# Moving the pauses of a gather queue to the borders of its work units

## The reference, cut to what matters

```
q, k, v = x @ Wq + bq, x @ Wk + bk, x @ Wv + bv      # 4 heads of 32
attn    = einsum('nhc,mhc->hnm', q, k) / sqrt(32)
alpha   = softmax(attn where adj != 0)               # over the neighbours m of node n
out     = einsum('hnm,mhc->nhc', alpha, v)
x_r     = x @ Ws + bs
beta    = sigmoid([out, x_r, out - x_r] @ Wb)
result  = layernorm(x + beta * x_r + (1 - beta) * out)
```

## Time and profile before

| | us |
|---|---|
| median of 3 runs (lowest, highest) | 1948.49 (1945.45, 1970.56) |
| profiled execution | 1964.78 |
| its span in the trace | 1962.9 |
| busy: POOL, DVE, PE, ACT | 1174.4, 1310.3, 1164.9, 839.9 |
| first and last gather on POOL, start | 66.5, 1936.1 |
| last result store on POOL, start | 1953.0 |

### The profile page before, as it was taken

The page is one execution under the profiler, slowest core; times in us unless marked ns, Lnnn a source line. Parts: engine busy times, 40 slices in busy tenths (PEclk is TensorE's granted clock), DMA queues, the critical chain, the costliest instruction groups (busy, mean ns, idle before and its releaser), DMA issues.

```text
span 1962.9 us, 20126 instructions
## 1 busy us (share of the span) xinstructions
PE 1164.9 (59%) x4696; PEld 680.4 (35%) x4696; DVE 1310.3 (67%) x3389; ACT 839.9 (43%) x1595; POOL 1174.4 (60%) x1711
## 2 busy tenths in 40 slices
PE   7322746657574756466655657756766668444553
PEld 5101433334342334233323334423423334233342
DVE  5876878666756776557656468757555677886564
ACT  2331443334643463344634348545635476431112
POOL 4454565566566656656566656565665665676664
PEclk9565677677776776667777578876667767666565
DMA  9947856666755776564866668776767778433331
GB/s 334 354 164 199 318 198 233 214 233 223 293 197 183 258 271 234 216 218 161 342 230 215 247 243 294 265 258 247 252 217 278 249 255 280 140 89 96 94 89 57
DMA packets 130037, 438.70 MB, mean 223 GB/s; under 512 B 26567, under 2 KB 61198, under 8 KB 97150
## 3 DMA queue, kind: packets, MB, share of 16 engines
q1 hardware_dynamic: 76510, 297.15, 41.1%
q0 software_dynamic: 52832, 136.07, 22.5%
q10 hardware_dynamic: 576, 4.19, 0.5%
HBM read 417.93 MB, written 19.44 MB: 223 GB/s over the span
## 4 chain that ended last, share of the span: by engine, by line
POOL 34%; issue 24%; DVE 13%; DMA 13%; PE 7%; DVEq 4%; another core or an unknown queue 3%; ACT 2%; SPq 1%; ACTq 0%; POOLq 0%
POOL s_kv L799 31%; DMA s_kv<-kv_rows,s_rec_in 11%; DVE s_raw L1248 2%; DVE s_kv L1246 2%; PE s_acc L1001 1%; DVEq L1296 1%; DVE s_wtop L1295 1%; POOL node_records L766 1%; POOL out_rows L775 1%; ACT s_mask L1023 1%; DVEq L1443 1%; DVE s_kv L1272 1%; DVE s_d_max L1454 1%; PE s_ps_key L889 1%
## 5 line engine op out<-in xcount | busy, mean ns | idle before, releaser
L799 POOL DMA_INDIRECT s_kv<-kv_rows,s_rec_in x1023 | 1024.3, 1001 | 700.6 <-DMA s_kv<-kv_rows,s_rec_in 340.6
L829 PE MATMUL s_ps_w<-s_mask,s_bit_w 128*128 128x512 bf16 x1008 | 374.6, 521 | 332.4 <-ACT s_mask L1023 233.8
L1023 ACT ACTIVATE s_mask<-s_adj_in 128x2048 bf16<-128x2048 f32 x252 | 478.2, 1900 | 114.5 <-DMA s_adj_in<-in_adj 66.7
L1001 PE MATMUL s_acc<-s_kv,ident 128*128 128x128 f32 x2032 | 321.3, 330 | 109.9 <-DVE s_kv L1272 62.8
L1001 PEld LDWEIGHTS s_acc<-s_kv,ident 128*128 128x128 f32 x2032 | 312.2, 244 | 137.4 <-DVE s_kv L1272 77.3
L829 PEld LDWEIGHTS s_ps_w<-s_mask,s_bit_w 128*128 128x128 bf16 x1008 | 111.3, 120 | 559.1 <-ACT s_mask L1023 294.9
L1246 DVE TENSOR_TENSOR s_kv<-s_kv,s_ps_q 128x1536 f32<-128x1536 f32 (+15 forms) x76 | 147.1, 1935 | 235.2 <-DMA s_kv<-kv_rows,s_rec_in 224.3
L1272 DVE TENSOR_TENSOR s_kv<-s_kv,s_ps_q 128x1536 f32<-128x1536 f32 (+15 forms) x76 | 146.7, 1931 | 17.9 <-ACT s_ps_q L1062 10.1
L1062 ACT ACTIVATE s_ps_q<-s_sc 128x56 f32<-128x56 f32 (+17 forms) x76 | 16.7, 220 | 318.4 <-DVE s_sc L1262 218.5
L1248 DVE TENSOR_REDUCE s_raw<-s_kv 128x48 f32<-128x1536 f32 (+15 forms) x76 | 147.1, 1935 | 5.6
L1050 ACT COPY s_xs<-s_ps_x 128x128 f32<-128x128 f32 x63 | 16.6, 264 | 288.7 <-remote 160.4
(11 more groups left out here) (281 smaller groups left out, 1563.2 us busy)
## 6 DMA issues: line engine op xcount, KB each, us to landing
s_adj_in<-in_adj SPq DMA_DIRECT2D x248, 1024.0 KB
s_kv<-kv_rows,s_rec_in POOLq DMA_INDIRECT x1023
kv_rows<-s_kv SPq DMA_DIRECT2D x16, 512.0 KB, 7.6
s_rec_in<-node_records SPq DMA_DIRECT2D x55, 106.0 KB
s_kv<-in_x_cols SPq DMA_DIRECT2D x4, 1024.0 KB, 8.4
s_adj_in<-in_adj ACTq DMA_DIRECT2D x4, 1024.0 KB
s_d_in<-in_x_cols SPq DMA_DIRECT2D x8, 512.0 KB
s_d_v<-kv_rows SPq DMA_DIRECT2D x8, 512.0 KB
```

What stands on the lines that cost most here:

```text
L799: nc.gpsimd.indirect_dma_start(out=kv[0:n, START[k] + s], out_offset=None, in_=kv_dram[:, :], in_offset=bass.IndirectOffsetOnAxis(ap=rec_i ...
L829: last = nc.tensor.matmul(w[:], bit_w[:, slab], mask[:, k % 2, s * WORD:(s + 1) * WORD], start=False, stop=(slab == SLABS - 1))
L1001: last = nc.tensor.matmul(acc[:, c * D:(c + 1) * D], ident[:], kv[:, START[k] + s, D:2 * D], start=(s == 0), stop=(s == plain(k) - 1))
L1023: nc.scalar.activation(mask[:, q % 2], adj_in[:, q % ADJ_RING], ACT.Sign, accum_out=edges[:, t, h:h + 1]).then_inc(masked, 1)
```

## The change

The pauses get other places. A unit is cut into `PIECES[k]` = ceil(HELD[k] / 14) pieces of nearly the same size, and POOL considers a pause only ahead of a piece (and, as before, ahead of a scatter and of a store): it pauses where the piece would not fit in what is left of 14. No unit has over 28 gathers, so a unit has one or two pieces.

```
--- before.py
+++ after.py
@@ -80,7 +80,7 @@
 NODE_AT = D + TOP
 DEGREE_MAX = 1023
 GATHER_US = 1.3
-RUN = 12
+RUN = 14
 SCAN_US = 15.0
 LEAD = 4
 BEHIND = 6
@@ -114,6 +114,14 @@
 
 
 HELD = [plain(k) + (k in FOLD_UNITS) for k in range(len(UNITS))]
+PIECES = [-(-s // RUN) for s in HELD]
+
+
+def piece_at(k, s):
+    return next((-(-(HELD[k] - s) // (PIECES[k] - i)) for i in range(PIECES[k])
+                 if s == sum(HELD[k] // PIECES[k] + (j < HELD[k] % PIECES[k]) for j in range(i))), 0)
+
+
 WINDOW_OF = {t: w for w, tiles in enumerate(WINDOWS) for t in tiles}
 
 
@@ -794,7 +802,8 @@
                     col, n = LIST_AT + first_slot(p, c) + s, rows_with(p, first_slot(p, c) + s)
                     if s == plain(k):
                         col, n = FOLD_AT, P
-                    pause_after(1)
+                    if piece_at(k, s):
+                        pause_after(piece_at(k, s))
                     begun["last"] = (k, s)
                     nc.gpsimd.indirect_dma_start(
                         out=kv[0:n, START[k] + s], out_offset=None, in_=kv_dram[:, :],
```

## The result

The change made the kernel slower: 2019.62 us (median of 4 runs, 1984.46 to 2042.13) against 1957.38 (median of 4 runs of the kernel before beside it, 1945.45 to 1970.56), ratio 1.020 with a 95% interval of 1.013 to 1.028. So the change costs time beyond the noise; whether it is more than 2% is open in this measurement. The forecast was 1898 us and a range that ended at 1940. The profiled execution of after took 1984.46 us, its span is 1982.6 us, 19.7 us over the span of before.

What follows compares the result with a forecast made beforehand. POOL, issuing transfers or pausing, was taken as the bound. Savings of 54.6 us where DVE waits and 12 at the end, less 14 for dearer borders, gave 52 us less: 1898 us from the 1948.5 median, range 1864 to 1940.

Steps and rivals of the forecast that it cites:

- 108 pauses, ten of them free: POOL's pauses go from 97 to 108; ten have later transfers issued or an already awaited gather, costed at nothing.
- The prices: Each POOL pause costed by its place with the old kernel's mean prices: 280.6 us in place of 371.3.
- 280.6 and 14: Forecast pause cost, plus 14 us back because borders behind a store, nearer the adjacency burst, cost 2.5 for 1.79 us.
- direct borders: Pauses at the border of two units with nothing issued in between, priced at 3.54 us each up to 1660 us.
- behind a store: Border pauses with one store issued after the unit's last gather, priced at 1.79 us, 2.5 for 19 of them.
- place does not matter: Rival: only transfers issued since count; direct pauses cost 4.17 us, a store takes off 1.30; 1916 us, chance 0.16.
- burst rival: Rival: shorter units put borders into SP's adjacency loads, 5.67 us direct, 5.56 behind a store; 1997 us, chance 0.08.
- POOL's lead: From 1447 to 1884 us POOL gets up to 21.5 us ahead, sparing DVE 12 us of its wait at the end.
- Nobody but POOL's own transfers holds POOL up for long: Reading of the old profile: POOL either issues, 1.30 us a transfer, or pauses.
- DVE takes it all: In three stretches where DVE waited for gathers 197.1 us, POOL's whole 54.6 us saving shortens the run.
- DVE, or the scan behind it, takes over: Rival: DVE's waits vanish and its list work comes into the open; half the gain stays, 1930 us, chance 0.14.
- The page's rule: Opposing rule: every wait for a landing pays about 2.0 us fixed, 2.3 us per 128 KB gather, wherever it stands.

Runs made afterwards that it cites:

- every 14: The kernel before with RUN = 14, a pause at every fourteenth transfer (83 pauses for 97): 1903.47 us, 0.971 times before.
- borders 12: The changed kernel with RUN = 12, 126 pauses, in two versions: border pauses behind the store 1.016 times before, ahead of it 1.029.
- one back: The kernel before, same 97 pauses, each waiting for the gather before the last, so one can still be in flight: 1.056 times before.

## Why the prediction was wrong

*108 pauses, ten of them free.* Right. The ten cost 0.3 us together.

*The prices.* Their sum was right within 6 us, if an idle time is cut at the landing: 280.6 and 14 make 294.6 us, measured 300.7. Uncut, as the forecast had measured the kernel before (371.3), the same idle times come to some 379 us, since the waits for records and slots stand in them. By class, up to 1660 us, cut at the landing: inside units 26 at 4.30 us (forecast 4.62), direct borders 25 at 4.22 (3.54), behind a store 32 at 1.84 (1.79 for 13, 2.5 for 19), and 24.4 us later (18.2). The "place does not matter" rival had 4.17 us for direct borders and units, which fits, but 2.87 behind a store, which does not: a store in between is worth 2.4 us, not 1.30. Of the burst rival a small part came: 0.68 us on 25 direct borders, 17 us, in line with the busy DMA engines at 885 us; its price of 5.67 us did not.

*POOL's lead.* "Right" was to be DVE's wait for gathers near 165 us; it is 104.6 us. "Wrong" was to be POOL's pauses down by 60 us or more with the end hardly moved, and that came, with the end later.

*The step that failed* is "Nobody but POOL's own transfers holds POOL up for long", carried over to the changed kernel, with "DVE takes it all" built on it. I priced a pause only as time that POOL loses. The term missing from my sum is what a full pause gives to the other engines; I put it at nothing, without a reason. It measured +85 us of other waits in the first trace of after and +169 in the second, against 67 us of forecast gain. What went wrong in the plan is not the number of transfers between two pauses (14 at most in pieces, as the rule says) but what a pause behind a store waits for: the gather issued before the store, and not the store. The cheapest class of the earlier trace rows was cheap because it did not wait for the queue to run empty (ahead of the store the pauses cost 65 us more together), and the change raised it from 9 pauses to 32 up to 1660 us. Between two moments with nothing in flight there were at most 24 transfers in before and 37 in after, and over 16 of them 5 times before, 15 times after.

*The rivals.* "DVE, or the scan behind it, takes over" named the right side: the chain goes from POOL to DVE and PE. Its mechanism was not this one (DVE's busy time is what it was, 1311.6 us, and PE's is lower, 1137.5 us), and it had no way to come out slower.

*The page's rule.* The Trainium skill, "DMA: Bandwidth & Descriptors", "Anatomy of one DMA - SWDGE (gpsimd) path", would have made 11 more pauses cost 25 us. The late direct pauses agree with it again (2.19 us for its 2.3), but all pauses together became 63 us cheaper; that the span grew by about as much (19.7 us) is chance.

**Shown**: at the same cost of pauses, 300 us, other waits are 25 us where a pause falls at every fourteenth transfer and 108 to 193 us where most stand behind stores (after), and putting after's border pauses ahead of the stores makes it faster. Beyond every 14, fewer or shorter full pauses make the others' work later by more than they save. **Argued only**: that it is the truly empty queue that counts, and not just how long POOL stands idle. For it speak after against every 14, with 16 and 6 flights over 25 us at the same idle time, and the table, where at most 8 such flights go with 13 to 34 us of other waits and 9 and more with 93 to 602. But the bound of 25 us was chosen afterwards, and in the three pairs with like numbers of pauses (after and its version ahead of the store, borders 12, before and one back) the idle time changed too, by 65, 63 and 159 us. **Not shown**: that the slow gaps and the 29.65 us of ACT are late loads of instructions. For it speaks only the cause "issue", with one instruction at a time; against it, the instruction packets named above. **Open**: what holds the other engines up; why 15 transfers (9 flights over 25 us, 161 us) do so much worse than 14 (6 flights, 25 us) and no worse than after; why after spread from 1984 to 2042 us on one chip; and what made three of four executions of the pause ahead of the store longer than the traced one.

## What to carry to other kernels

Before you move or cheapen a wait, ask what the rest of the chip does while it lasts. Look up what each pause leaves in flight, and count the longest stretch without a full pause before and after the change. Where pauses serve to empty a queue, first try their number with their form kept: RUN from 12 to 14, one constant, gained what the new rule was meant to gain. And cut an idle time at the moment at which its first cause was over, or a price per pause also contains the waits of others.

## What the runs showed that I had not expected

- Other engines can be held up while POOL's queue of gathers does not run empty: PE at one instruction in 1.4, 2.1 or 2.8 us (16 such matmuls took 1.87 us otherwise), ACT still for 29.65 us, DVE in the kernel before for 20.57 us, and in these three places all free again 1 to 4 us behind POOL's last transfer in it.
- In this kernel there is an edge between 14 and 15 transfers without a pause: 0.971 and 1.017 times before, then 1.048 at 16 and 1.086 at 24.
- Shortening each of the same 97 pauses by one gather made them 159 us cheaper and the other waits 251 us longer (275 for 24).
